# Turning the shared groups' last controls ahead of the sorted groups in a two-layer network kernel with a routed mixture of experts

## The chip, the core and the metric

The kernel runs on one core of a Trainium2 chip, as one program. The core's engines run side by side and meet at semaphores: TensorE (PE: matrix products and transposes into PSUM), VectorE (DVE), ScalarE (ACT: table functions), GpSimd (POOL: here it issues the indirect DMAs, which gather and scatter rows by an index) and SyncE (SP: here it issues all other DMAs, strictly in its program's order). The metric is the device time of one execution in microseconds (us).

## The reference

The input is 8 sequences of 512 tokens with 128 features. Four blocks follow each other, each added to its input: an attention, a gated feed-forward, a linear attention with three small MLPs, and a mixture of experts (`_L1_ffn_ref`). All of the change lies in the last:

```python
logits = gelu(xf @ router_w1 + router_b1) @ router_w2 + router_b2
topk_p, topk_i = top_k(softmax(logits), 2)            # of 8 experts, p renormalised
v, integrated = 0, xf
for _ in range(2):
    ctx = concat([integrated, v])
    x_sh, v_sh = inl(gelu(ctx @ shared_w1 + b) @ shared_w2 + b, integrated, v, mu)
    x_r, v_r   = sum over the token's 2 experts e of  p_e * inl(gelu(ctx @ w1[e] + b) @ w2[e] + b, integrated, v, mu)
    x_next, v_next = sw * x_sh + (1 - sw) * x_r, sw * v_sh + (1 - sw) * v_r
    halt = sigmoid(gelu(integrated @ halt_w1 + b) @ halt_w2 + b)
    integrated, v = integrated + halt * (x_next - integrated), v + halt * (v_next - v)
out = xf + integration_weight * (gelu(integrated @ refine_w1 + b) @ refine_w2 + b)

def inl(ctrl, x, v, mu):                              # ctrl: the three controls a, b, g of a token
    v_next = sigmoid(a) * v - softplus(b) * (x - mu)
    return x + 0.1 * sigmoid(g) * v_next, v_next
```

## The kernel before

The mixture works on groups of 512 tokens (four tiles of 128). A *shared* group S holds tokens in their own order and applies the shared weights; a *sorted* group E holds tokens that were scattered by expert into memory (`slots`), and each of its four tiles uses one expert's weights. The tokens are cut in two halves h = 0, 1, and there are two iterations it = 1, 2. `STAGES` sets the order of the 56 groups: S(h0,it1) 0 to 3, E(h0,it1) 4 to 13, S(h1,it1) 14 and 15, **E(h1,it1) 16 to 25**, S(h1,it1) 26 and 27, S(h0,it2) 28 to 31, **E(h0,it2) 32 to 41**, S(h1,it2) 42 to 45, **E(h1,it2) 46 to 55**. The three E stages in bold follow shared groups; `LATE_STARTS` holds their first groups, 16, 32 and 46. "Place 1", "2" and "3" below are the turns from shared to sorted groups at 16, 32 and 46.

A group passes these steps, and each engine runs its list of steps in an order written out by loops over `s`:

- SP `load_in` reads a sorted group's tokens from `slots` (the first three of a stage at once, as soon as the scatters of that half are through); `load_w1` reads its experts' first weights, four DMAs, and waits until the hidden layer of the sorted group four before has been through ACT (semaphore a_g); `store` writes a sorted group's results to `moved`.
- PE `g_turn` ("T") transposes the group's tokens, ACT `turned` copies them out of PSUM. PE `g_hidden` ("H") multiplies by the first weights, ACT `hidden_gelu` applies the gelu.
- PE `g_control` multiplies by the second weights: one or two units a group, in two pairs of PSUM banks used in turn, so that a unit waits for ACT to have read the unit before last. DVE `copy_b` copies the b controls out of PSUM and ACT `gates`, which waits for that copy, applies tanh to the others.
- ACT `soft` makes the softplus of the b controls of two groups at once. It is a table load, Exp, Ln and a second table load.
- DVE `elements` (waits for the softplus) and `moved_on` make the group's results. For a shared group they also write the token's own state.

Around this POOL moves rows. For each of the phases 0, 1 and 2 it runs over the 16 tiles of a half: `gather` (two indirect DMAs) fetches a token tile's two expert results from `moved`, DVE `update` adds them to the token's state, and `scatter` (two indirect DMAs) sends the new state to `slots` for the next sorted stage. Phase 0 begins once the results of all sorted groups to 13 are stored, phase 1 once those to 25 are. In the last stage `slots_back` sends sorted results back by index, four DMAs a group, and waits for that group's `moved_on`. `UPDATES` places the updates at the ends of DVE's steps s, from s = 16, 30 and 45 on.

`turn_steps(s)` says where in step s PE and ACT do which T and H. SP's loop is

```python
for s in range(-1, NG + 2):
    if is_e(s + 5):
        load_w1(s + 5)
        if not any(f <= s + 5 < f + 3 for f in LATE_STARTS):
            load_in(s + 5)
    if is_e(s - 2) and by_slots(s - 2):
        store(s - 2)
```

so at s = 15 it stands at `load_w1(20)`, `load_in(20)`, `store(13)`.

Of the kernel before, what the change touches and what calls it, by code (L numbers as in the profile page):

```python
# [96 lines left out]
GROUPS = []  # L97
# [9 lines left out]
def turned_in(g):  # L107

    return GROUPS[g][0] == "E" or GROUPS[g][2] == 2
# [34 lines left out]


LATE_STARTS = (16, 32, 46)


def dve_parts(g):
# [3 lines left out]

    if not turned_in(g) or g == FIRST_E or any(f <= g < f + 3 for f in LATE_STARTS) or GROUPS[g - 5][0] == "S" or GROUPS[g][2] == 2:
        return ()
# [7 lines left out]
def turn_steps(s):  # L163

    if s < FIRST_E:
        f = FIRST_E
        return [], [("T", f), ("T", f + 1), ("H", f), ("T", f + 2), ("H", f + 1)] if s == f - 1 else []  # L170
    turned = lambda g: g < NG and turned_in(g)
    middle = [("H", s + 2)] if turned(s + 2) and s + 2 not in LATE_STARTS and s + 1 not in LATE_STARTS else []
    end = [("T", s + 3)] if turned(s + 3) and s + 3 not in LATE_STARTS and s + 2 not in LATE_STARTS else []
    if s + 2 in LATE_STARTS:
        end = [("T", s + 2)]
    if s + 1 in LATE_STARTS:
        middle = [("H", s + 1)]
        end = [("T", s + 2), ("H", s + 2), ("T", s + 3)]
    return middle, end
# [76 lines left out]
def build(nc, x, early, late, experts, seconds, out):  # L256
    with ExitStack() as ctx:
# [538 lines left out]
        def _(dve):  # L796
# [209 lines left out]
            for t in range(NSEQ):  # L1006
                k, s = t % 2, with_b(t)
# [275 lines left out]
                r_norm(t)  # L1283
            weights(0)
            for s in range(1, NG + 2):
                if s < NG:
                    copy_b(s, 0)
                if s >= 2:
                    elements(s - 2)
                if s < NG:  # L1290
                    if unit_count(s) == 2:
                        copy_b(s, 1)
                if s >= 2:
                    moved_on(s - 2)
                if s == 2:
                    routes(1)
                    hots(1)
                if s == 3:
                    sort(1)
                if s == 4:  # L1300
                    weights(1)
                for what, g in turn_steps(s)[1]:
                    if what == "T":
                        turned(g)
                for ph, m in UPDATES.get(s, ()):
                    update(ph, m)
# [21 lines left out]
        def _(act):  # L1328
# [141 lines left out]
            for t in range(NSEQ):  # L1470
                k, s = t % 2, with_b(t)
# [131 lines left out]

            for s in range(NG + 1):
                middle, end = turn_steps(s)
                if s % 2 == 0 and s >= 2:
                    soft(s // 2 - 1)
                if s < NG:
                    gates(s, 0)
                if s == 1:  # L1610
                    r_gelu(HSEQ + 2)
                for what, g in middle:
                    hidden_gelu(g)
                if s < NG and unit_count(s) == 2:
                    gates(s, 1)
                if s == 0:
                    shares(0)
                    r_evacuate(HSEQ, 0)
                    r_evacuate(HSEQ + 1, 0)
                    r_gelu(HSEQ)  # L1620
                    r_evacuate(HSEQ + 2, 1)
                    r_gelu(HSEQ + 1)
                    r_evacuate(HSEQ + 3, 1)
                if s == 1:
                    r_gelu(HSEQ + 3)
                if s == 3:
                    shares(1)
                for what, g in end:
                    if what == "T":
                        turned(g)  # L1630
                    else:
                        hidden_gelu(g)
# [682 lines left out]
```

How the kernel before makes its waits and increments, by code:

```python
def need(eng, sem, value):  # L216
    if not isinstance(value, int) or value > 0:
        eng.wait_ge(sem, value)
# [2 lines left out]
def settle(eng, S):  # L222
    eng.wait_ge(S["row_in0"], 16)
# [242 lines left out]
        @block.sync  # L468
        def _(sp):
            for t in range(NSEQ // 2):
                sp.dma_start(X[:, 2 * t * TILES:2 * (t + 1) * TILES, :], x_in[t]).then_inc(S[f"row_in{t}"], 16)
            sp.dma_start(WE[:, FIRST_N:], early[:, FIRST_N:]).then_inc(S["w_early"], 16)
            sp.dma_start(WL[:, :], late).then_inc(S["w_late"], 16)
            sp.wait_ge(S["p_set"], 1)
            for d in (*X1d, *X2d):
                flat = d.rearrange("(p a) d -> p (a d)", p=P)
                for a in range(0, flat.shape[1], 4 * SEQ):
                    n = min(4 * SEQ, flat.shape[1] - a)
                    sp.dma_start(flat[:, a:a + n], zeros[:, 0:n]).then_inc(S["z_fill"], 16)
            sp.wait_ge(S["w_late"], 16)
            sp.wait_ge(S["z_fill"], 16 * (Z_FILLS - 1))
            sp.dma_start(X1d[1].rearrange("(p a) d -> p a d", p=P)[:, :, P], wl("spare"), allow_slow_non_contiguous=True)\
                .then_inc(S["z_fill"], 16)
            sp.wait_ge(S["ln_rs"], 14)
            sp.dma_start(EW2, seconds).then_inc(S["w_late"], 16)
            def experts_of(h, i):
# [5 lines left out]
            def load_in(g):  # L495
                _, h, it, i = GROUPS[g]
                e = EXP_AT[g]
                sp.wait_ge(SC[h], 16 * 2 * HT * it)
                if e == 4:
                    sp.wait_ge(S["r_y"], NSEQ)
```

## Time and profile before

| | us |
|---|---|
| median of 3 runs (991.86, 994.6, 995.5) | 994.6 |
| the profiled execution | 991.68 |
| its span | 989.9 |
| busy: PE, DVE, ACT, POOL | 782.1, 577.9, 566.4, 488.1 |
| busy share: PE, DVE, ACT, POOL | 79%, 58%, 57%, 49% |

The span is what the instructions cover; the 1.8 us beside it lie before the first and after the last. Every number of an instant counts from the span's start. No engine is busy throughout, so what counts is which one is waited for at each place.

### The profile page before, as it was taken

To read this page: it belongs to the slowest core of one execution; us is meant where nothing else is said; L and a number is where in the kernel's file an instruction comes from. 1 tells how busy PE (TensorE), PEld (TensorE's weight loads), DVE (VectorE), ACT (ScalarE), POOL (GpSimd) and SP (SyncE) were. 2 spreads that over 40 slices of the span, in tenths; PEclk is the share of its full clock that TensorE was granted. 3 is DMA by queue.
4 is the path that set the end of the run, shared out by engine and by line. 5 is a ranking of instruction groups with operands and counts; after the bars stand their busy time and mean duration, and the time that the engine had idled before them with its cause. 6 is when DMAs were issued, how large, how long until landed. Compare 5 with 4: busy or idle time off the path is not lost.

```text
span 989.9 us, 13034 instructions
## 1 busy us (share of the span) xinstructions
PE 782.1 (79%) x3904; PEld 535.8 (54%) x3904; DVE 577.9 (58%) x1438; ACT 566.4 (57%) x1003; POOL 488.1 (49%) x436
## 2 busy tenths in 40 slices
PE   7799997587888877999999856575576668877477
PEld 4588886444444435767676644454344444544255
DVE  6622333648888682222434588658566877586655
ACT  5744444544445304635544539877666898788532
POOL 1411202335554486224434777537777775467750
PEclk9999999799999997999999969887898999888789
DMA  9940000000000000000000535657557664633124
GB/s 344 423 136 1 0 1 1 1 1 0 1 1 1 0 1 0 1 1 1 1 1 27 186 92 152 207 158 226 166 175 238 202 191 146 196 121 101 48 78 128
DMA packets 75921, 92.90 MB, mean 94 GB/s; under 512 B 24032, under 2 KB 61920, under 8 KB 73808
## 3 DMA queue, kind: packets, MB, share of 16 engines
q1 hardware_dynamic: 65248, 65.87, 20.7%
q0 software_dynamic: 10464, 25.66, 8.1%
q10 hardware_dynamic: 144, 0.59, 0.2%
q8 instruction: 31, 0.51, 0.2%
q14 instruction: 34, 0.28, 0.1%
HBM read 45.95 MB, written 46.13 MB: 93 GB/s over the span
## 4 chain that ended last, share of the span: by engine, by line
PE 46%; DVE 16%; POOL 11%; ACT 11%; issue 9%; DMA 5%; POOLq 0%; DVEq 0%; SPq 0%; ACTq 0%
PE PS L1945 7%; PE PS L1954 6%; POOL tokens L693 4%; POOL KEEP L770 3%; PE PS L1752 3%; PE PS L1723 3%; PE PS L1864 3%; PE PS L1960 3%; PE PS L1832 3%; POOL slots L684 3%; PE PS L1713 2%; DMA KEEP<-moved,small 2%; DVE TEMP L961 2%; PE PS L1660 2%; PE PS L2058 2%
## 5 line engine op out<-in xcount | busy, mean ns | idle before, releaser
L2069 PE MATMUL PS<-TEMP,KEEP 128*128 x320 | 116.9, 508 | 36.9 <-ACT TEMP L1569 30.4
L770 POOL DMA_INDIRECT KEEP<-moved,small x96 | 104.4, 1087 | 69.9 <-issue 35.4
L675 POOL DMA_INDIRECT slots<-KEEP,small x96 | 101.1, 1053 | 47.2 <-issue 27.4
L2069 PEld LDWEIGHTS PS<-TEMP,KEEP 128*128 128x128 f32 x320 | 66.5, 223 | 65.1 <-issue 50.7
L1509 ACT ACTIVATE KEEP<-PS,TEMP 128x512 f32<-128x512 f32 x96 | 63.5, 690 | 58.0 <-PE PS L1945 57.1
L1569 ACT ACTIVATE TEMP<-PS 128x512 f32<-128x512 f32 (+2 forms) x92 | 51.5, 561 | 78.3 <-DVE TEMP L1180 77.7
L621 POOL TENSOR_TENSOR KEEP<-KEEP 128x1024 f32<-128x1024 f32 x32 | 63.7, 2005 | 53.6 <-PE PS L1864 51.8
L1945 PE MATMUL PS<-TEMP_R 128*128 128x512 f32 x288 | 77.1, 422 | 4.2 <-POOL TEMP_R L715 3.8
L2091 PE MATMUL PS<-KEEP,TEMP 128*64 128x128 f32 x480 | 40.2, 308 | 42.2 <-issue 19.1
L1864 PE MATMUL PS<-KEEP,TEMP 128*128 128x512 f32 x128 | 62.7, 619 | 9.3 <-DVE TEMP L961 8.2
L1945 PEld LDWEIGHTS PS<-TEMP_R 128*128 128x128 f32 x288 | 56.2, 198 | 20.1 <-POOL TEMP_R L715 4.2
L1180 DVE COPY TEMP<-PS 128x256 f32<-128x256 f32 (+1 forms) x92 | 43.8, 477 | 37.9 <-PE PS L2058 19.4
L2091 PEld LDWEIGHTS PS<-KEEP,TEMP 128*64 128x64 f32 x480 | 29.7, 154 | 64.4 <-issue 25.3
L1582 ACT ACTIVATE KEEP<-PS,TEMP 64x128 f32<-64x128 f32 x160 | 57.7, 360 | 9.4 <-PE PS L2091 7.6
L1954 PE MATMUL PS<-KEEP,TEMP 128*128 128x512 f32 x128 | 56.3, 593 | 0.0
L2058 PE MATMUL PS<-WL,KEEP 128*128 128x257 f32 (+1 forms) x128 | 47.7, 510 | 6.4 <-ACT TEMP L1569 6.3
L1666 PE MATMUL PS<-WL,TEMP 128*128 128x128 f32 x256 | 39.9, 297 | 16.0 <-DMA TEMP<-slots 13.1
L1273 DVE SCALAR_TENSOR_TENSOR KEEP<-KEEP,small 128x256 f32<-128x256 f32 (+1 forms) x64 | 26.5, 414 | 39.7 <-DMA KEEP<-moved,small 33.5
L1127 DVE TENSOR_SCALAR TEMP_R<-PS,TEMP 128x512 fp32r<-128x512 f32 x16 | 12.0, 751 | 62.3 <-PE PS L1954 62.3
L961 DVE TENSOR_TENSOR TEMP<-PS,KEEP 128x1024 f32<-128x1024 f32 x32 | 38.9, 1216 | 15.0 <-PE PS L1864 13.1
L1666 PEld LDWEIGHTS PS<-WL,TEMP 128*128 128x128 f32 x256 | 31.6, 151 | 27.8 <-issue 21.0
L715 POOL TENSOR_TENSOR TEMP_R<-KEEP,TEMP_R 128x512 fp32r<-128x512 f32 x8 | 8.7, 1090 | 73.3 <-ACT KEEP L1501 73.3
(275 smaller groups left out, 1877.5 us busy)
## 6 DMA issues: line engine op xcount, KB each, us to landing
slots<-LX SPq DMA_DIRECT2D x14, 1024.0 KB, 25.8
moved<-LX SPq DMA_DIRECT2D x20, 512.0 KB, 3.3
TEMP<-slots SPq DMA_DIRECT2D x20, 512.0 KB, 3.8
TEMP<-experts SPq DMA_DIRECT2D x80, 64.5 KB
TEMP<-seconds SPq DMA_DIRECT2D x1, 3072.0 KB
TEMP<-early SPq DMA_DIRECT2D x1, 2765.0 KB, 12.0
TEMP<-experts SPq DMA_DIRECT2D x80, 32.5 KB
TEMP<-slots SPq DMA_DIRECT2D x10, 258.0 KB, 3.8
```

The lines of the kernel that those rows point to most:

```text
L621: pool.tensor_tensor(o, kk, vv, ALU.mult).then_inc(S["c1_kv"], 1)
L675: pool.indirect_dma_start(dst, bass.IndirectOffsetOnAxis(ap=pos[:, h, 2 * m + k:2 * m + k + 1], axis=0), src, None).then_inc(SC[h], 16)
L770: pool.indirect_dma_start(G[:, n % 4, k, 0:w], None, src, bass.IndirectOffsetOnAxis(ap=pos[:, h, 2 * m + k:2 * m + k + 1], axis=0))\
L961: dve.tensor_tensor(qm[:, c % 2].rearrange("p (h v k) -> p h v k", h=HEADS, v=HD), acc, q, ALU.mult)\
L1509: act.activation(d_G[:, k, SEQ * c:SEQ * (c + 1)], PS[:, 2 + c, :], ACT.Gelu_apprx_tanh, bias=bias)\
L1666: last = pe.transpose(PS[:, bank, P * j:P * (j + 1)], src[:, j], eye)
L1864: last = pe.matmul(PS[:, 4 + 2 * (c % 2) + h, :], we("tril"), kv[:, c % 2, SEQ * h:SEQ * (h + 1)], start=True, stop=True)
L1945: last = pe.matmul(PS[:, 2 + c, :], CWr[:, pw, at:at + P], hTr[:, k, px], start=n == 0, stop=n == 2)
L1954: last = pe.matmul(PS[:, 6 + k, :], w2[:, P * c:P * (c + 1)], d_G[:, k, SEQ * c:SEQ * (c + 1)], start=c == 0, stop=c == HC - 1)
L2058: last = pe.matmul(PS[:, bank + j, 0:n], HS[:, hs_slot(g), col:col + P], wl("sw2")[:, 0:n], start=True, stop=True)
L2069: last = pe.matmul(o, hT[:, e % 3, P * j:P * (j + 1)], EW2[:, 384 * (j % 2):][:, bass.ds(at[j], n)], start=True, stop=True)
L2091: last = pe.matmul(PS[side:side + EHID, bank, part], W1[:, e % 4, j, 1 + EHID * a:1 + EHID * (a + 1)], xTs[:, x % 2, a, part], start=a == ...
```

## The change

At each late start f, the two shared groups f-2 and f-1 are finished before the sorted groups are turned. On ACT, `soft` of that pair moves from the start of step f into step f-1, behind the gates of group f-1. On DVE, `elements` and `moved_on` of f-2 and f-1, which stood in steps f and f+1 between the copies of sorted controls, stand at the start of step f ahead of those copies. At 16 and 32 (`TURNED_LAST`) T and H of the first sorted groups move behind both control units of group f-1 on PE and behind the softplus on ACT; at 46 T and H keep their places on PE, and on ACT the copy of 47 and what follows come behind the softplus. SP and POOL keep their lists word for word.

```diff
 LATE_STARTS = (16, 32, 46)
+TURNED_LAST = (16, 32)
...
     end = [("T", s + 3)] if turned(s + 3) and s + 3 not in LATE_STARTS and s + 2 not in LATE_STARTS else []
-    if s + 2 in LATE_STARTS:
+    if s + 2 in LATE_STARTS and s + 2 not in TURNED_LAST:
         end = [("T", s + 2)]
-    if s + 1 in LATE_STARTS:
+    if s + 1 in TURNED_LAST:
+        f = s + 1
+        if GROUPS[f][2] == 1:
+            end = [("T", f), ("T", f + 1), ("H", f), ("T", f + 2), ("H", f + 1)]
+        else:
+            end = [("T", f), ("H", f), ("T", f + 1), ("H", f + 1), ("T", f + 2)]
+    elif s + 1 in LATE_STARTS:
         middle = [("H", s + 1)]
         end = [("T", s + 2), ("H", s + 2), ("T", s + 3)]
...
             for s in range(1, NG + 2):
+                if s in LATE_STARTS:
+                    for g in (s - 2, s - 1):
+                        elements(g)
+                        moved_on(g)
+                in_turn = s >= 2 and s not in LATE_STARTS and s - 1 not in LATE_STARTS
                 if s < NG:
                     copy_b(s, 0)
-                if s >= 2:
+                if in_turn:
                     elements(s - 2)
                 if s < NG:
                     if unit_count(s) == 2:
                         copy_b(s, 1)
-                if s >= 2:
+                if in_turn:
                     moved_on(s - 2)
...
-                if s % 2 == 0 and s >= 2:
+                if s % 2 == 0 and s >= 2 and s not in LATE_STARTS:
                     soft(s // 2 - 1)
...
                 if s < NG and unit_count(s) == 2:
                     gates(s, 1)
+                if s + 1 in LATE_STARTS:
+                    soft(s // 2)
```

ACT at place 1, before. The first row is `gates` of group 14 (both units); L1599 is the copy of a turned group (16, 17, 18), L1582 the gelu of a sorted group (16, 17), the other 128x2x129 rows are the gates of group 15, and the last four rows are the softplus of 14 and 15.

```order
L1569 ACTIVATE TEMP<-PS 128x2x129 x2
L1599 ACTIVATE KEEP<-PS,WL 128x512
L1569 ACTIVATE TEMP<-PS 128x2x129
L1582 ACTIVATE KEEP<-PS,TEMP 64x128 x4
L1569 ACTIVATE TEMP<-PS 128x2x129
L1599 ACTIVATE KEEP<-PS,WL 128x512
L1582 ACTIVATE KEEP<-PS,TEMP 64x128 x4
L1599 ACTIVATE KEEP<-PS,WL 128x512
L1554 ACT_TABLE_LOAD
L1558 ACTIVATE LX<-TEMP 128x1024
L1560 ACTIVATE LX<-LX 128x1024
L1561 ACT_TABLE_LOAD
```

ACT at place 1, in the changed kernel, whose lines are 12 higher on this engine:

```order
L1581 ACTIVATE TEMP<-PS 128x2x129 x4
L1566 ACT_TABLE_LOAD
L1570 ACTIVATE LX<-TEMP 128x1024
L1572 ACTIVATE LX<-LX 128x1024
L1573 ACT_TABLE_LOAD
L1611 ACTIVATE KEEP<-PS,WL 128x512 x2
L1594 ACTIVATE KEEP<-PS,TEMP 64x128 x4
L1611 ACTIVATE KEEP<-PS,WL 128x512
L1594 ACTIVATE KEEP<-PS,TEMP 64x128 x4
```

The softplus has moved ahead of the first copy of a sorted group, and so ahead of the gelu of group 16 (the first row of four).

ACT at place 2, before: the first row is the gates of group 30, L1599 and L1601 are the two copies of a turned group of iteration 2 (32, then 33, then 34), the single 128x514 rows are the gates of group 31, and then comes the softplus of 30 and 31.

```order
L1569 ACTIVATE TEMP<-PS 128x514 x2
L1599 ACTIVATE KEEP<-PS,WL 128x512
L1601 ACTIVATE KEEP<-PS 128x512
L1569 ACTIVATE TEMP<-PS 128x514
L1582 ACTIVATE KEEP<-PS,TEMP 64x128 x4
L1569 ACTIVATE TEMP<-PS 128x514
L1599 ACTIVATE KEEP<-PS,WL 128x512
L1601 ACTIVATE KEEP<-PS 128x512
L1582 ACTIVATE KEEP<-PS,TEMP 64x128 x4
L1599 ACTIVATE KEEP<-PS,WL 128x512
L1601 ACTIVATE KEEP<-PS 128x512
L1554 ACT_TABLE_LOAD
```

The same place in the changed kernel:

```order
L1581 ACTIVATE TEMP<-PS 128x514 x4
L1566 ACT_TABLE_LOAD
L1570 ACTIVATE LX<-TEMP 128x1024
L1572 ACTIVATE LX<-LX 128x1024
L1573 ACT_TABLE_LOAD
L1611 ACTIVATE KEEP<-PS,WL 128x512
L1613 ACTIVATE KEEP<-PS 128x512
L1594 ACTIVATE KEEP<-PS,TEMP 64x128 x4
L1611 ACTIVATE KEEP<-PS,WL 128x512
L1613 ACTIVATE KEEP<-PS 128x512
L1594 ACTIVATE KEEP<-PS,TEMP 64x128 x4
```

All copies and gelus of the sorted groups 32 to 34 now stand behind both gates of 31 and behind the softplus.

DVE at place 2 in the changed kernel, from the last update of step 31 to the first copies of group 32 (L1280 and L1283 are an update, L1218 to L1229 `elements`, L1240 to L1253 `moved_on`, once for group 30; the same eight rows follow for 31):

```order
L1280 SCALAR_TENSOR_TENSOR KEEP<-KEEP,small 128x256
L1283 SCALAR_TENSOR_TENSOR KEEP<-KEEP,small 128x256
L1218 TENSOR_SCALAR small<-TEMP,small 128x4
L1220 SCALAR_TENSOR_TENSOR small<-TEMP,small 128x4 x2
L1222 SCALAR_TENSOR_TENSOR TEMP<-LX,TEMP 128x512
L1224 SCALAR_TENSOR_TENSOR TEMP<-TEMP,KEEP 128x4x128
L1229 TENSOR_TENSOR TEMP<-TEMP,KEEP 128x512
L1240 SCALAR_TENSOR_TENSOR LX<-TEMP 128x4x128
L1242 SCALAR_TENSOR_TENSOR LX<-TEMP,LX 128x4x128
L1253 SCALAR_TENSOR_TENSOR KEEP<-LX,small,KEEP 128x128 x4
```

What stood after `copy_b` of group 32 now stands ahead of it; ahead of all this, the update (1,0) at the end of step 30 still stands in front of `copy_b` of group 31, as before.

## Rows read from the trace of the kernel before

**Rows 1.** The chain that ended last: start, us, what; pieces at the three places.

```profile
640.34 3.25 DMA TEMP<-slots
...
652.22 4.08 DMA moved<-LX
...
657.11 1.45 POOL KEEP L770
...
751.32 1.94 PE PS L1666 x8
...
884.58 1.12 POOL tokens L693
```

**Rows 2.** POOL by stretches: us, busy (instructions), granted clock, DMA share, GB/s.

```profile
657.10:746.30 89.20, 69.97 (x64) 0.85 0.57 179
...
884.50:956.70 72.20, 56.19 (x53) 0.82 0.25 78
```

**Rows 3.** Timeline of ACT at place 1: start, us, instruction, idle before it.

```profile
640.21 0.89 ACT L1569 ACTIVATE TEMP<-PS 128x258 f32<-128x258 f32 x2
644.84 0.69 ACT L1599 ACTIVATE KEEP<-PS,WL 128x512 f32<-128x512 f32 x1 [3.74 <-PE PS L1666]
...
647.62 1.49 ACT L1582 ACTIVATE KEEP<-PS,TEMP 64x128 f32<-64x128 f32 x4 [0.22 <-PE PS L2091]
...
653.20 1.28 ACT L1554 ACT_TABLE_LOAD   x1
...
657.95 0.60 ACT L1569 ACTIVATE TEMP<-PS 128x512 f32<-128x512 f32 x1
```

**Rows 4.** Timeline of SP's DMA queue at place 1.

```profile
649.66 1.88 SPq L520 DMA_DIRECT2D TEMP<-experts  x4
...
652.22 0.61 SPq L527 DMA_DIRECT2D moved<-LX  x1
```

**Rows 5.** Timeline of PE at place 1.

```profile
635.49 1.14 PE L2058 MATMUL PS<-WL,KEEP 128*128 128x257 f32 x4 [0.36 <-ACT TEMP L1569]
643.72 1.08 PE L1666 MATMUL PS<-WL,TEMP 128*128 128x128 f32 x4 [7.09 <-DMA TEMP<-slots]
644.60 1.92 PE L2058 MATMUL PS<-WL,KEEP 128*128 128x257 f32 x4
```

**Rows 6.** Timeline of DVE at place 1.

```profile
649.01 0.68 DVE L1235 SCALAR_TENSOR_TENSOR LX<-TEMP,LX 128x512 f32<-128x512 f32 x1
```

**Rows 7.** Timeline of DVE at place 2.

```profile
754.21 0.48 DVE L1273 SCALAR_TENSOR_TENSOR KEEP<-KEEP,small 128x256 f32<-128x256 f32 x1 [2.01 <-DMA KEEP<-moved,small]
...
755.86 0.42 DVE L1180 COPY TEMP<-PS 128x256 f32<-128x256 f32 x1 [0.65 <-PE PS L2058]
...
757.68 0.68 DVE L1222 TENSOR_TENSOR TEMP<-TEMP,KEEP 128x512 f32<-128x512 f32 x1
```

**Rows 8.** Timeline of ACT at place 2.

```profile
756.32 0.60 ACT L1569 ACTIVATE TEMP<-PS 128x514 f32<-128x514 f32 x1 [2.43 <-DVE TEMP L1180]
...
762.25 1.49 ACT L1582 ACTIVATE KEEP<-PS,TEMP 64x128 f32<-64x128 f32 x4 [1.20 <-PE PS L2091]
...
774.76 0.60 ACT L1569 ACTIVATE TEMP<-PS 128x512 f32<-128x512 f32 x1 [1.26 <-DVE TEMP L1180]
...
778.99 1.28 ACT L1554 ACT_TABLE_LOAD   x1
```

**Rows 9.** Timeline of ACT at place 3.

```profile
857.70 0.69 ACT L1599 ACTIVATE KEEP<-PS,WL 128x512 f32<-128x512 f32 x1
...
877.15 1.28 ACT L1554 ACT_TABLE_LOAD   x1
```

**Rows 10.** Timeline of DVE at place 3.

```profile
866.24 0.23 DVE L1211 TENSOR_SCALAR small<-TEMP,small 128x4 f32<-128x4 f32 x1 [3.45 <-ACT TEMP L1560]
...
871.17 0.35 DVE L1273 SCALAR_TENSOR_TENSOR KEEP<-KEEP,small 128x128 f32<-128x128 f32 x1
...
880.62 0.69 DVE L1215 SCALAR_TENSOR_TENSOR TEMP<-LX,TEMP 128x512 f32<-128x512 f32 x1 [1.18 <-ACT LX L1560]
```

## The prediction

> **What bounds the kernel now.** The page comes first: no engine is over 79% busy, so an average decides nothing. The chain that ended last comes next, and at the three places it names what is waited for [rows 1]. At place 1 it goes from the first load of sorted tokens (640.34) over PE to the store of group 13 (652.22, 4.08 us to landing), and from there to POOL's first gather at 657.11. At place 2 it comes out of a load into T of group 32 (751.32) and then follows ACT and PE. In the last stage it enters POOL, whose first `slots_back` is at 884.58. The stretches of POOL say what lies between: 64 indirect DMAs in 89.2 us from 657.1 to 746.3, and 53 in 72.2 us from 884.5 to 956.7 [rows 2]. That is 1.39 and 1.36 us each; the timeline of POOL shows 0.30 us between neighbours and nothing longer in both stretches. POOL issues them as fast as it can. So whatever delays its first gather of phase 0, or its first `slots_back`, is paid at the end in full. Between 751 and 846 ACT, PE and DVE hand work to each other every few tenths; only a wait inside that round counts there. So the question is, place by place: when does the gelu of 16 end (place 1), when does ACT get to softplus (16) of groups 32 and 33 (place 2), and when to softplus (23) of 46 and 47 (place 3)?
>
> **Place 1.** PE waits 7.09 us for the sorted tokens [rows 5]. The change lets it do the units of group 15 in that time. The first waits for the gates of 14, which ACT begins at 640.21 and has done at 640.6 and 641.1 [rows 3]. A unit takes 1.14 us at the higher clock; a first one after a long idle time took 1.92 [rows 5]. The two end at 641.8 and 643.0, or at 642.6 and 644.4. T of 16 follows, its data landing at 643.7. DVE copies the b controls (0.42), does the two operations of `elements(13)` (1.4), copies again; the gates of 15 (0.39 each) end at 644.5 to 645.3. `moved_on(13)` ends near 645 to 645.9 and not at 649.01 + 0.68 = 649.7 [rows 6]. That is the gain that one sees first, 4 us or more.
>
> ACT, however, now does softplus (7) first: from 653.20 to 657.95 it took 4.75 us [rows 3]. So the copy of 16 starts at 649.3 to 650.0 and not at 644.84. It takes 0.69, H of 16 then takes 0.7 to 1.1 with its hand-overs, and the gelu 1.49: it ends at 652.2 to 653.5. Before it ended at 647.62 + 1.49 = 649.11. SP is queued behind that: `load_w1(20)` waits for this gelu and started 0.55 us after it, at 649.66, and behind it in SP's list stands `store(13)`, at 652.22 [rows 4]. SP's list is unchanged, so the result of 13 that is ready 4 us earlier lies there while SP waits 3.1 to 4.4 us longer for experts' weights that nobody needs yet. POOL's first gather waits for that store. It starts at 660.2 to 661.5. I take **+3.5 us**, since the clock falls part of the way. Nothing gives it back up to 746: POOL is full. The updates wait for gathers, so DVE and ACT come later by the same amount. What remains of DVE's freed time, the `elements` and `moved_on` of 15 out of the way of step 17, is worth nothing here, as POOL sets the pace.
>
> **Place 2**, counted from its own load. The units of 31 can run from 749.1 on, in the wait for the load at 751.32. But DVE's next act is not their copy. It is the update (1,0), which waits for a gather until 754.21, and its two operations end at 755.2 [rows 7]. `copy_b` of 31 started at 755.86 before, and starts at 755.2 now. The wait that the change wants to fill has another wait in front of it: it wins 0.6 us. From there I count ACT from the first gates of 31 to softplus (16).
>
> Before: from 756.32 to 778.99, 22.67 us [rows 8]. Its waits are 0.41, 0.45, 1.20 (for H), 1.26 (for DVE's copy) and 0.45, together 3.8 (the timeline gives each in brackets, the two longest are in the rows), so 18.9 is work. The 1.18 us of copies of 32 lay earlier, in a wait.
> After: it starts 755.7. The work is 18.9 + 1.18 = 20.1. The waits are: 1.8 from one gate of 31 to the other, since the `elements(29)` between the two copies hold DVE for 2.4 (from 755.86 to 757.68 + 0.6 in rows 7); 1.2 each for H of 32 and of 33, since nothing else stands between copy and gelu any more; 0.2 and 0.4 and 0.4 in step 32; 0.8, 0.1 and 0.5 in step 33, where DVE has no elements left. Together 6.6. It ends at 755.7 + 20.1 + 6.6 = 782.4: **+3.4 us**. DVE does not make it worse: `moved_on(29)` and the updates (1,1) and (1,2) end at 762.4, four blocks of 2.3 us for 30 and 31 follow, and `copy_b` of 32 is reached at 772, when PE gives it. PE idles near 10 us before H of 32. If it is then at the lower clock, as the L2058 of 1.92 us against 1.14 was [rows 5], H and T lose up to 1.5 us: upper end +5. At the lower end the small waits that I added vanish: +2.5. Nothing waits for a DMA in DVE up to 838, so no slack swallows it.
>
> **Place 3.** On ACT softplus (22) now begins where the copy of 47 did, at 857.70 [rows 9], and Ln is ready at 861.1. DVE then runs both groups at once: from `elements(44)` at 866.24 to its first update at 871.17 are 4.93 us with a copy of 0.34 in it [rows 10], so 4.7 a group; from 861.2 it is busy until 870.6, and only then copies the controls of 46, which PE had ready at 867.2. ACT before: from 857.70 to softplus (23) at 877.15 are 19.45 us [rows 9], with waits of 1.20, 1.61 and 0.45. After: the same work, with waits of 1.2 (H of 47), 3.6 (DVE's copy, from 867.5 to 871.05), 0.5 and 0.4. That is 5.7 against 3.3: **+2.4 us**, between +1.5 and +3.5. `elements(46)` started at 880.62 when Ln was there, and starts at 883.0. `moved_on(46)` ended at 884.2, and POOL's `slots_back(46)` followed at 884.58 [rows 1]: no slack. The gathers ahead of it on POOL wait for updates which keep their times.
>
> **Sum:** 3.5 + 3.4 + 2.4 = 9.3 us, and by the ends 3.1 + 2.5 + 1.5 = 7.1 to 4.4 + 5 + 3.5 = 12.9. A gain is excluded at place 1 by SP's order and at 2 by DVE's. Against the profiled execution's own 991.68 this is 1001.0. The median of the runs shown is 2.9 above that execution, whose time is their lowest; on the median the sum gives 1003.9. I take 1003.5.
>
> **A rule weighed.** A table load takes 1.28 us, and the softplus with two of them, Exp and Ln ends 4.75 us after it began, when the gates of 16 start [rows 3]; two drains would not fit into that. The Trainium skill (ScalarE: Activation LUTs, What ACT_TABLE_LOAD costs) adds a drain of about 1.38 us to every switch, 2.66 together. By that the softplus would be 7.5 us, and place 1 alone would cost 2.8 us more, a sum of 12.1. The row decides here.
>
> **Rivals.**
> 1. *The store is not held, so place 1 does not lose.* If SP reaches `store(13)` before the gelu of 16, because load and store stand otherwise than I read them or the first wait is met by other work, POOL starts when `moved_on(13)` is done: 4.7 us earlier and not 3.5 later. The sum is then 9.3 - 8.2 = +1.1, 995.7 on the median: no slower. For it speaks that the result is really earlier. Against it speak 649.66 right behind 649.11 and SP's unchanged list. It decides whether the first gather comes before or after 657.1 in the trace.
> 2. *The gather of update (1,0) lands before 751*, so that copies, gates and softplus (15) run in the wait for the load. ACT gets to the copy of 32 about 4.7 us earlier than I count, at 758.8, and place 2 gives -1.3. The sum is +4.6, 999.2 on the median. Against it: gathers and the first loads share the DMA engines there, and DVE waited 2.01 us for it [rows 7].
> 3. *The loss is larger:* PE's clock is lower at each restart, and at place 3 DVE's late copies also delay the updates ahead of POOL's gathers. All upper ends and 2 us for the gathers: +15, 1009.6.
> 4. *Everything is absorbed* or the freed engines win somewhere that I do not see, above all in DVE's steps 17, 33 and 47, which are shorter now by 4 to 5 us each. If two of these three reached the chain, some 9 us would come back and it would be level, or up to 5 us faster with all three.
>
> **How the numbers follow.** A measurement of this kernel tells about 0.5%, 5 us, from no change. The forecast (+7 to +13) has a chance of 0.64, rival 1 of 0.10, rival 2 of 0.08, rival 3 of 0.10, rival 4 of 0.07; the table rule has 0.01. Slower by over 0.5%: 0.64 + 0.10 + 0.01 and half of rival 2, 0.79. Within 0.5%: rival 1, half of 2, and 0.02 of 4, 0.16. Faster: 0.05. The range takes the forecast with the 3 us between single runs of one kernel and reaches to rivals 2 and 3: 997 to 1009.
>
> **What would show it.** POOL's first gather of `moved` at 660 to 661.5, with 64 DMAs behind it without a gap; SP's four expert loads straight after a gelu that ends at 652 to 653.5; `moved_on(13)` done near 645 and waiting. At place 2, ACT idle from the gates of 30 until some 4.4 us after T of 32 began, and softplus (16) 31 us after that T instead of 27.7. At place 3, DVE without a pause from Ln to the copy of 46, and 2.4 us more from the second gates of 45 to softplus (23). I am wrong if the first gather comes before 657 or if the stretches after it are shorter.

## The result, and the profile after

The changed kernel takes 1005.43 us (median of 4 runs, 1002.69 to 1009.32), the kernel before 995.05 us in the same comparison: a ratio of 1.0115, with a 95% interval of 1.0084 to 1.0146. The change costs some 11 us. The profiled execution took 1002.69 us with a span of 1000.9 us, so 11.0 us more than the one of before.

Place 1 first: SP's DMA queue of the changed kernel. These rows answer to [rows 4].

```profile
644.50 0.61 SPq L534 DMA_DIRECT2D moved<-LX  x1
655.33 1.88 SPq L527 DMA_DIRECT2D TEMP<-experts  x4
657.32 0.52 SPq L517 DMA_DIRECT2D TEMP<-slots  x1
657.89 0.62 SPq L534 DMA_DIRECT2D moved<-LX  x1
```

Between the stores of 12 and of 13 SP stands 10 us before the expert load of group 20. Its two neighbours on the timelines, ScalarE and VectorE of the changed kernel, say why, and what was ready meanwhile; they answer to [rows 3, 6].

```profile
646.63 1.28 ACT L1566 ACT_TABLE_LOAD   x1
...
651.38 1.26 ACT L1611 ACTIVATE KEEP<-PS,WL 128x512 f32<-128x512 f32 x2
653.29 1.49 ACT L1594 ACTIVATE KEEP<-PS,TEMP 64x128 f32<-64x128 f32 x4 [0.65 <-PE PS L2105]
...
665.96 0.60 ACT L1581 ACTIVATE TEMP<-PS 128x512 f32<-128x512 f32 x1 [9.08 <-DVE TEMP L1187]
```

```profile
646.11 0.68 DVE L1242 SCALAR_TENSOR_TENSOR LX<-TEMP,LX 128x512 f32<-128x512 f32 x1
...
662.10 0.69 DVE L1229 TENSOR_TENSOR LX<-TEMP,KEEP 128x512 f32<-128x512 f32 x1 [6.86 <-DMA moved<-LX]
...
665.24 0.69 DVE L1187 COPY TEMP<-PS 128x512 f32<-128x512 f32 x1
```

`moved_on(13)` is over at 646.8. The gelu of 16 comes behind softplus (7) and ends at 654.8. Only then does SP issue the expert load, then the load of 20, and at 657.89 the store of the result that has lain ready for 11 us. POOL's first gather waits for it, as the timeline and two stretches of POOL show (they answer to [rows 2]; columns: us, busy with instructions, granted clock of TensorE, DMA share, GB/s).

```profile
662.82 0.98 POOL L777 DMA_INDIRECT KEEP<-moved,small  x1 [25.18 <-DMA moved<-LX]
```

```profile
662.70:749.80 87.10, 67.67 (x64) 0.75 0.58 183
895.20:967.40 72.20, 55.84 (x53) 0.82 0.25 77
```

The reader is to see three things here. The first gather is 5.7 us later than before. The 64 DMAs behind it have no gap, but take 87.1 us and not 89.2. And there is a wait that the prediction does not have: `elements(15)` writes the buffer from which the store of 13 reads, so VectorE stands 6.86 us, and ScalarE behind it 9.08 us. It adds nothing to the chain: VectorE's first update, at 666.96, still waits 1.03 us for its gather.

Place 2, ScalarE and TensorE of the changed kernel, answering to [rows 8] and the T row of [rows 1]:

```profile
754.23 0.60 ACT L1581 ACTIVATE TEMP<-PS 128x514 f32<-128x514 f32 x1 [0.67 <-DVE TEMP L1187]
758.28 0.60 ACT L1581 ACTIVATE TEMP<-PS 128x514 f32<-128x514 f32 x1 [3.46 <-DVE TEMP L1187]
760.70 0.60 ACT L1581 ACTIVATE TEMP<-PS 128x514 f32<-128x514 f32 x1 [1.82 <-DVE TEMP L1187]
...
769.32 1.49 ACT L1594 ACTIVATE KEEP<-PS,TEMP 64x128 f32<-64x128 f32 x4 [2.07 <-PE PS L2105]
...
785.75 1.28 ACT L1566 ACT_TABLE_LOAD   x1
```

```profile
758.00 1.04 PE L1680 MATMUL PS<-WL,TEMP 128*128 128x128 f32 x8
767.29 1.97 PE L2105 MATMUL PS<-KEEP,TEMP 128*64 128x128 f32 x16 [8.26 <-ACT KEEP L1613]
...
791.83 2.66 PE L2083 MATMUL PS<-TEMP,KEEP 128*128 x4 [2.59 <-ACT TEMP L1581]
794.41 1.62 PE L2105 MATMUL PS<-KEEP,TEMP 128*64 128x128 f32 x16
```

Place 3, ScalarE, answering to [rows 9]:

```profile
865.83 1.28 ACT L1566 ACT_TABLE_LOAD   x1
...
873.83 1.49 ACT L1594 ACTIVATE KEEP<-PS,TEMP 64x128 f32<-64x128 f32 x4 [2.08 <-PE PS L2105]
...
879.24 0.60 ACT L1581 ACTIVATE TEMP<-PS 128x512 f32<-128x512 f32 x1 [2.72 <-DVE TEMP L1187]
...
887.96 1.28 ACT L1566 ACT_TABLE_LOAD   x1
```

Single executions of one kernel differ by several microseconds (35 runs of the kernel before on one chip: 990.3 to 1000.7), and part of that has arisen by 630 us, ahead of every edit: softplus (6) starts at 635.46 before and 636.80 after, and between 635.5 and 639.9 over all the kernels below, though nothing ahead of it differs. So I compare stretches between fixed points of the timelines, not absolute times. A is from softplus (6) to the first gather; B from there to the first gather of the second half; C to softplus (16); D to softplus (21); E to softplus (23). In us:

| profiled execution | A | B | C | D | E | ratio of times (95%) |
|---|---|---|---|---|---|---|
| before | 21.65 | 89.47 | 32.41 | 65.26 | 32.90 | |
| changed | 26.02 | 87.17 | 35.76 | 66.64 | 35.57 | 1.0115 (1.0084 to 1.0146) |
| place 1 alone | 26.24 | 86.37 | 31.83 | 65.27 | 31.51 | 1.0016 (0.9993 to 1.0040) |
| place 2 alone | 21.89 | 89.26 | 37.80 | 66.65 | 32.90 | 1.0052 (1.0033 to 1.0072) |
| place 3 alone | 22.77 | 88.13 | 32.62 | 65.27 | 35.58 | 1.0024 (0.9998 to 1.0050) |
| changed, store first | 15.97 | 88.76 | 37.57 | 66.55 | 35.55 | 1.0012 (0.9991 to 1.0033) |
| before, store first | 17.97 | 89.86 | 32.47 | 65.28 | 31.33 | 0.9960 (0.9936 to 0.9985) |
| changed, update (1,0) behind | 26.11 | 87.01 | 33.59 | 65.26 | 35.64 | 1.0087 (1.0054 to 1.0120) |
| changed, 18 fillers | 26.24 | 86.50 | 38.19 | 65.26 | 33.95 | 1.0113 (1.0081 to 1.0145) |
| changed, 10 fillers | 26.04 | 86.92 | 34.85 | 67.78 | 35.57 | 1.0122 (1.0085 to 1.0159) |
| place 3, softplus alone | 21.60 | 89.42 | 32.62 | 65.26 | 36.82 | 1.0029 (1.0007 to 1.0051) |
| place 3, VectorE alone | 21.76 | 89.53 | 32.45 | 65.31 | 39.51 | 1.0104 (1.0057 to 1.0150) |
| place 1 and store first | 16.71 | 88.66 | 31.88 | 65.30 | 31.35 | 0.9941 (0.9909 to 0.9973) |

From softplus (6) on the changed kernel's span is 9.66 us longer: A and B together 2.07, C 3.35, D 1.38, E 2.67, and what lies behind 0.19. The other 1.34 us of the 11.0 stand ahead of softplus (6).

### The profile page after: what moved, and what is told of

Read it like the earlier page. It is cut to its first block, busy times and chain, and to the rows that moved or that the text cites. A ratio compares the mean times of both kernels' runs of the same rounds, so it can differ in the third digit from the quotient of the medians.

```text
span 1000.9 us, 13034 instructions
## 1 busy us (share of the span) xinstructions
PE 794.6 (79%) x3904; PEld 544.6 (54%) x3904; DVE 579.5 (58%) x1438; ACT 567.0 (57%) x1003; POOL 484.5 (48%) x436
## 4 chain that ended last, share of the span: by engine, by line
PE 48%; DVE 16%; ACT 14%; issue 10%; POOL 9%; DMA 3%; SPq 0%; POOLq 0%; DVEq 0%; ACTq 0%
PE PS L1959 7%; PE PS L1968 6%; POOL tokens L700 4%; PE PS L1766 3%; PE PS L1737 3%; PE PS L1878 3%; POOL KEEP L777 3%; PE PS L1974 3%; PE PS L1846 3%; PE PS L2083 3%; PE PS L1727 2%; DVE TEMP L968 2%; ACT L1566 2%; DMA KEEP<-moved,small 2%; PE PS L1674 2%
## 5 line engine op out<-in xcount | busy, mean ns | idle before, releaser
L2083 PE MATMUL PS<-TEMP,KEEP 128*128 x320 | 123.2, 530 | 29.8 <-ACT TEMP L1581 25.4
L777 POOL DMA_INDIRECT KEEP<-moved,small x96 | 99.8, 1039 | 79.2 <-issue 36.3
L682 POOL DMA_INDIRECT slots<-KEEP,small x96 | 103.5, 1079 | 47.3 <-issue 26.8
L2083 PEld LDWEIGHTS PS<-TEMP,KEEP 128*128 128x128 f32 x320 | 69.1, 231 | 60.3 <-issue 46.5
L2105 PE MATMUL PS<-KEEP,TEMP 128*64 128x128 f32 x480 | 42.9, 324 | 53.4 <-ACT KEEP L1613 18.0
L2105 PEld LDWEIGHTS PS<-KEEP,TEMP 128*64 128x64 f32 x480 | 32.0, 164 | 75.6 <-ACT KEEP L1613 32.0
L1280 DVE SCALAR_TENSOR_TENSOR KEEP<-KEEP,small 128x256 f32<-128x256 f32 (+1 forms) x64 | 26.5, 414 | 38.0 <-DMA KEEP<-moved,small 32.1
L1878 PEld LDWEIGHTS PS<-KEEP,TEMP 128*128 128x128 f32 x128 | 22.6, 195 | 40.1 <-issue 30.9
L2072 PEld LDWEIGHTS PS<-WL,KEEP 128*128 128x128 f32 x128 | 27.4, 227 | 31.1 <-ACT TEMP L1581 18.2
## 6 DMA issues: line engine op xcount, KB each, us to landing
TEMP<-seconds SPq DMA_DIRECT2D x1, 3072.0 KB, 11.3
```

What stands on the lines that cost most here:

```text
L682: pool.indirect_dma_start(dst, bass.IndirectOffsetOnAxis(ap=pos[:, h, 2 * m + k:2 * m + k + 1], axis=0), src, None).then_inc(SC[h], 16)
L777: pool.indirect_dma_start(G[:, n % 4, k, 0:w], None, src, bass.IndirectOffsetOnAxis(ap=pos[:, h, 2 * m + k:2 * m + k + 1], axis=0))\
L1878: last = pe.matmul(PS[:, 4 + 2 * (c % 2) + h, :], we("tril"), kv[:, c % 2, SEQ * h:SEQ * (h + 1)], start=True, stop=True)
L2072: last = pe.matmul(PS[:, bank + j, 0:n], HS[:, hs_slot(g), col:col + P], wl("sw2")[:, 0:n], start=True, stop=True)
L2083: last = pe.matmul(o, hT[:, e % 3, P * j:P * (j + 1)], EW2[:, 384 * (j % 2):][:, bass.ds(at[j], n)], start=True, stop=True)
L2105: last = pe.matmul(PS[side:side + EHID, bank, part], W1[:, e % 4, j, 1 + EHID * a:1 + EHID * (a + 1)], xTs[:, x % 2, a, part], start=a == ...
```

## Experiments

**One place at a time.** The three parts of the change (order of transposes, VectorE's elements, softplus) get a list of places each; for place 1 alone all three hold 16, for place 2 alone 32, and for place 3 alone the first is empty and the other two hold 46.

```diff
-TURNED_LAST = (16, 32)
+TURNED_LAST = (16,)
+DVE_FIRST = (16,)
+SOFT_FIRST = (16,)
...
-                if s in LATE_STARTS:
+                if s in DVE_FIRST:
                     for g in (s - 2, s - 1):
...
-                in_turn = s >= 2 and s not in LATE_STARTS and s - 1 not in LATE_STARTS
+                in_turn = s >= 2 and s not in DVE_FIRST and s - 1 not in DVE_FIRST
...
-                if s % 2 == 0 and s >= 2 and s not in LATE_STARTS:
+                if s % 2 == 0 and s >= 2 and s not in SOFT_FIRST:
...
-                if s + 1 in LATE_STARTS:
+                if s + 1 in SOFT_FIRST:
```

> The new order at the start at group 16 alone; the starts at 32 and 46 as before. Theory of the store (the expert load that waits for the gelu of 16 stands ahead of the store of 13 in SP's queue, and the first gather waits for that store): the gelu of 16 ends 3 to 4.5 us later, the first gather is issued 4 to 5 us later than in the kernel before, POOL gives back about 2 us of it over the 64 gathers and scatters, as the changed kernel's trace shows, and the loads of 32 to 34 and the end come 2.5 to 4 us later: about 998.4 us. Rival, the clock (the longer silences of TensorE at a start bring it down to its lower level, and most of the 10 us comes from that at 32 and 46): nothing of place 1 reaches the end, 995 us. Before group 16 nothing differs; if softplus stands 1.3 us late from 600 us on here as well, that offset belongs to something else than the order.

Measured: 995.04 against 994.16 us, 1.6 us by the ratio, and not told apart from nothing. That is the time of the rival and not the 998.4 of the theory. The theory's own sign is there: A is 4.6 us longer, as expected. But B is 3.1 us shorter where 2 had been expected, so of the loss at the store 1.5 us are left, and in this execution even those are covered, by C (0.6 shorter) and by E (1.4 shorter, because TensorE's clock was higher there; see the last section).

> The new order at the start at group 32 alone. Theory of the blocked copies (the copy of 31 waits on VectorE behind the first update of the second half, and the copies, gelu and softplus of 32 wait behind it on ScalarE): softplus of pair 16 starts 3.4 us later than before, counted from the landing of the loads of 32, and with some matmuls at the lower clock behind it up to 1.4 us more is lost before the gates of 44: 998 to 1000 us. Rival (the loss at 32 is only there because place 1 moved the gathers and so the landing of the first update against the gates): the loss is under 1.5 us here, below 996.5.

Measured: 999.92 us, 5.2 us by the ratio. The loss at 32 is there without place 1, and it is larger than in the changed kernel's trace: C by 5.4 us, where 3.4 had been expected, and D by 1.4.

> The new order of softplus and VectorE's elements at the start at group 46 alone; TensorE's order is the one before everywhere. Theory: from the second gates of 45 to softplus of pair 23 it takes 2.4 to 2.7 us more and POOL's last part is bound by what it gets from VectorE: 997.3 to 998 us. Rival (the last part is bound by POOL's issues, which give the 2.5 us back): 995 us.

Measured: 998.11 us, 2.4 us by the ratio, at the edge of what can be told from nothing; E is longer by 2.68. The three single losses add up to 9.2 us, inside the interval of the whole change (8.4 to 14.5).

**The store ahead of the expert load**, in the changed kernel and in the one before:

```diff
             for s in range(-1, NG + 2):
+                if s == 15:
+                    store(s - 2)
                 if is_e(s + 5):
...
-                if is_e(s - 2) and by_slots(s - 2):
+                if is_e(s - 2) and by_slots(s - 2) and s != 15:
                     store(s - 2)
```

> The changed kernel, with one step moved in SP's program: at turn 15 the store of group 13 is issued ahead of the expert load of group 20 (which waits for the gelu of 16) and of the load of 20. Theory of the store: it is issued right behind moved_on of 13, near 647 us instead of 657.9, the first gather follows near 652 instead of 662.8, VectorE's wait of the elements of 15 for the store's landing is gone, and the end moves by 8 to 11 us: 994.5 to 997.5 us. Rival (the late restart of TensorE and ScalarE at 16 is what costs, and the gathers only follow it): no gain, 1004 to 1006 us, whatever the store does. Between these, about 1001 us, if the first updates are then waited for by something else.

Measured: 995.74 us, ratio 1.0012 to before; that is 10 us less than the changed kernel (6.9 us less in the profiled execution, counted from softplus (6)). The timeline of POOL:

```profile
652.29 1.05 POOL L781 DMA_INDIRECT KEEP<-moved,small  x1 [13.74 <-DMA moved<-LX]
```

The first gather is 10.5 us earlier than in the changed kernel. The gelu of 16 is not: in both kernels it ends 18.0 us behind the start of softplus (6). So a late gelu makes late gathers only through SP's order, which holds the finished store behind the load that waits for that gelu; this is shown. Places 2 and 3 still lose: D and E as in the changed kernel, C 5.2 us against the kernel before, more than the 3.35 of the changed kernel and near the 5.4 of place 2 alone.

> The kernel before, with the same step moved in SP's program as in the run of the changed kernel with the store first: at turn 15 the store of 13 ahead of the expert load of 20. Theory of the store: the expert load's wait for the gelu of 16 held the store in the kernel before too, so the first gather comes near 652 us instead of 657.1, and the 64 gathers and scatters behind it end about 6 us earlier: 987 to 990 us. Rival (the sorted groups' own chain takes over as soon as POOL is ready sooner): 992 to 994 us.

Measured: 991.97 against 994.15 us, ratio 0.9960. That is the time of the rival: A is shorter by 3.7 us, and 5 had been expected. SP now waits for something else, as its timeline and VectorE's show:

```profile
647.10 1.44 SPq L519 DMA_DIRECT2D TEMP<-slots  x1
648.59 3.54 SPq L536 DMA_DIRECT2D moved<-LX  x2
652.70 1.90 SPq L529 DMA_DIRECT2D TEMP<-experts  x4
```

```profile
648.80 0.42 DVE L1191 COPY TEMP<-PS 128x256 f32<-128x256 f32 x1 [5.64 <-PE PS L2076]
...
651.09 0.68 DVE L1246 SCALAR_TENSOR_TENSOR LX<-TEMP,LX 128x512 f32<-128x512 f32 x1
```

The row x2 of SP joins the stores of 12 and 13. With the old order `moved_on(13)` ends at 651.8, since VectorE waits for control products of 15 that stand behind T of 16. The new order removes just that. Hence the next kernel.

**Place 1 in the new order, and the store first**: both diffs above together, 32 and 46 as in the kernel before.

> Both edits that the stretch at group 16 seems to want: the new order at the start at 16 alone (as in the run of place 1 alone) and SP's store of 13 ahead of the expert load of 20. Theory of the store: the new order has the last elements of 13 done 5 us earlier than the old one does (646 against 651 us), and only SP's order kept that from the gathers; so the first gather comes 16 us behind softplus of pair 6 (before 21.7, store first alone 18.0), the first gather of the second half 6 us earlier than before, and with the old order at 32 and 46 nothing of it is given back: 987 to 989 us, ratio 0.993 to 0.995. Rival (the place loses as much by TensorE's silence as the store gains): as with the store first alone, 992 us, ratio 0.998.

Measured: 988.27 against 994.87 us, ratio 0.9941: faster than the kernel before and the changed one. A and B together are 105.4 us (before 111.1, changed 113.2, store first alone 107.8). By these stretches one part of the change is a gain of 2.5 us, once SP lets it through. The times alone do not show that part: the intervals of this kernel and of the store first alone overlap (0.9909 to 0.9973, and 0.9936 to 0.9985).

**The update behind the copy of 31**, in the changed kernel:

```diff
-        UPDATES.setdefault(_at + ((_m + 1) // 2 if _ph == 2 else UPDATE_STEPS[_m]), []).append((_ph, _m))
+        UPDATES.setdefault(_at + ((_m + 1) // 2 if _ph == 2 else max(UPDATE_STEPS[_m], _ph == 1)), []).append((_ph, _m))
```

> The changed kernel, with one step moved on VectorE: the first update of the second half stands behind the copy of 31 (turn 31) instead of ahead of it (turn 30). Theory of the blocked copies: the copy of 31 no longer waits for the landing of that update's gather, the second wait of the gates of 31 loses most of its 3.5 us, TensorE's silence before the hidden product of 32 shrinks from 8.3 us to about 5, and softplus of pair 16 comes 3 to 4.5 us earlier against the first gather of that half (35.8 us behind it in the changed kernel): 1000.5 to 1002 us. Rival (order of softplus and copies on ScalarE alone costs the 3.4 us): no change, 1005 us.

Measured: 1000.53 us, ratio 1.0087, some 3 to 5 us less than the changed kernel. Timelines of ScalarE and TensorE:

```profile
755.90 0.60 ACT L1583 ACTIVATE TEMP<-PS 128x514 f32<-128x514 f32 x1 [2.23 <-DVE TEMP L1189]
```

```profile
765.05 1.98 PE L2107 MATMUL PS<-KEEP,TEMP 128*64 128x128 f32 x16 [6.17 <-ACT KEEP L1615]
```

C falls by 2.2 us, where 3 to 4.5 had been expected, and the second gates of 31 still wait 2.23 us of the 3.46. Of the 3.35 us 1.2 are left; H of 32 still takes 1.98 us, at the lower clock. And D falls back to 65.26, which I had not expected of this edit: the silence of TensorE is 2.1 us shorter, and the pairs behind stand 13.48 us apart again.

**The clock.** Over 786 to 842 us TensorE was granted full clock before, and 0.91 of it in the changed kernel. At H of 32 and the T behind it (767.29 to 771.20) it was granted 0.50, the lower of its two levels, 1.2 of 2.4 GHz. The stretch by windows, before and after (columns: us, busy with instructions, granted clock, DMA share, GB/s):

```profile
786.00:842.00 56.00, 43.56 (x227) 1.00 0.59 178
```

```profile
786.00:842.00 56.00, 45.99 (x236) 0.91 0.56 170
```

To test it I filled the silence ahead of H of 32 with work whose result is overwritten. It writes the bank of H of 32, once the gelus that read the bank are done.

```diff
+FILLED, FILLERS = (("H", 32),), 18
...
+            def filler(g):
+                x = HID_AT[g]
+                pe.wait_ge(S["a_g"], x - 1)
+                for _ in range(FILLERS):
+                    pe.matmul(PS[:, 2 + x % 2, 0:384], wl("gA"), wl("sw2")[:, 0:384], start=True, stop=True)
...
                 for what, g in end:
+                    if (what, g) in FILLED:
+                        filler(g)
```

> The changed kernel with 18 matmuls of 128 x 384 added on TensorE between the transposes and the hidden product of group 32, into a bank that the product overwrites; the output does not change. They take 7 us at the higher clock and fill most of the silence of 8.3 us. Theory of the clock (the silence brings TensorE to its lower level, the products of 32 and 33 take 1.97 instead of 1.09 us, and for four pairs of groups behind it the first control products take 2.7 to 2.9 instead of 1.55 us): these rows go back to 1.09 and 1.55 us, softplus of pairs 16 to 20 stand 13.5 us apart as before instead of 14.0, and 2 to 3.5 us come back: 1002 to 1003.5 us. Rival (the clock is off the path; the distance is set by VectorE's updates): 1005 us, and 14.0 us apart whatever the clock.

Measured: 1005.25 us, as the changed kernel. TensorE's timeline:

```profile
761.52 11.78 PE L2139 MATMUL PS<-WL 128*128 128x384 f32 x36
773.22 1.09 PE L2108 MATMUL PS<-KEEP,TEMP 128*64 128x128 f32 x16
```

The clock did what was expected: H takes 1.09 us, the pairs are 13.48 apart and D is 65.26. So D's 1.38 us are the clock's. But the 18 fillers took 11.8 us and not 7 (each shows as two records of 0.33 us), and the gelu of 32 waited 3.87 us for them instead of 2.07. C grew by 2.4 us, 1.8 of it that wait, which is more than D gave back.

> The changed kernel with 10 added matmuls between the transposes and the hidden product of group 32 in place of 18 (18 took 11.8 us, ran 3.6 us past the moment at which the product could start, and gave back in the clock what they cost). 10 take 6.5 us, inside the silence of 8.3 us. Theory of the clock: nothing is delayed, the products of 32 and 33 take 1.09 us, the pairs behind stand 13.5 us apart; softplus of pair 16 comes 34 us behind the first gather of the second half, not 35.8, and that of pair 21 another 65.3 us behind, not 66.6: 1001.5 to 1003.5 us. Rival (the lower clock at 32 costs only where it shows, under 1 us in all): 1004.5 us or more.

Measured: 1006.32 us, a time that the rival had given; nothing came back. The fillers took 6.6 us and delayed nothing, C is 0.9 us shorter, but D is 1.1 longer. TensorE's timeline at the second pair of sorted groups:

```profile
792.91 1.57 PE L2086 MATMUL PS<-TEMP,KEEP 128*128 x4 [2.58 <-ACT TEMP L1584]
795.43 1.98 PE L2108 MATMUL PS<-KEEP,TEMP 128*64 128x128 f32 x16 [0.95 <-ACT KEEP L1616]
797.33 2.93 PE L2086 MATMUL PS<-TEMP,KEEP 128*128 x4
```

H of 32 ran at the higher clock (1.09 us), but the clock fell all the same, 26 us behind it (granted 0.50 over 795.4 to 800.3), and that one pair took 15.75 us. The clock theory holds for what a low stretch costs (1.4 us in D, 0.9 in C). That filling most of the long silence is enough to save it is wrong. The 18 fillers, which left nothing of it, did keep the clock up to 842; each size was profiled once.

**Place 3 taken apart.** Softplus ahead, VectorE as before (`SOFT_FIRST = (46,)`, the others empty):

> At the start at group 46 softplus of pair 22 goes ahead on ScalarE as in the changed kernel, but VectorE keeps the order of before; the starts at 16 and 32 are those of before. Theory (the loss of 2.4 to 2.7 us at this start is VectorE's, which does both groups' elements ahead of the copy of 46): no loss here, within 1 us of before, 993.5 to 995.5 us, and softplus of pair 23 comes 33 us behind that of 21, not 35.6. Rival (it is ScalarE's order, softplus ahead of the copies of 46 and 47, which leaves TensorE silent): 35.6 us again, 996.5 to 998 us.

Measured: 997.09 us, ratio 1.0029; E is 36.82. My theory fell. It is not VectorE's order that costs: softplus ahead of the copies costs 3.9 us of E by itself. (By the times it is 2.9 us, 0.7 to 5.1.) ScalarE's timeline has the waits that this order brings, for H of 47 at the lower clock and then for two copies of VectorE:

```profile
867.76 1.49 ACT L1596 ACTIVATE KEEP<-PS,TEMP 64x128 f32<-64x128 f32 x4 [2.08 <-PE PS L2107]
...
872.32 0.60 ACT L1583 ACTIVATE TEMP<-PS 128x512 f32<-128x512 f32 x1 [1.87 <-DVE TEMP L1189]
...
878.96 0.60 ACT L1583 ACTIVATE TEMP<-PS 128x512 f32<-128x512 f32 x1 [2.34 <-DVE TEMP L1189]
```

VectorE ahead, softplus as before (`DVE_FIRST = (46,)`, the others empty):

> At the start at group 46 VectorE does the elements of 44 and 45 ahead of the copy of 46, but softplus of pair 22 stays behind the copies, gelus and gates on ScalarE where it was; 16 and 32 as before. Theory formed on the last run (softplus ahead of the copies of 46 and 47 is what costs here, 3.9 us by itself, and VectorE's order gives 1.2 us of that back): alone VectorE's order gains nothing, since its elements wait for the late softplus and the copy of 46 waits behind them: softplus of pair 23 comes 35 to 38 us behind that of 21 (before 32.9): 996.5 to 999 us. Rival (VectorE's order is the better one whatever ScalarE does): 31.5 to 33 us and 993 to 994.5 us.

Measured: 1003.68 us, ratio 1.0104, E 39.51: worse than expected. The copy of 46 waits behind elements that wait for a late softplus, and ScalarE stands 8.61 us:

```profile
876.98 0.60 ACT L1583 ACTIVATE TEMP<-PS 128x512 f32<-128x512 f32 x1 [8.61 <-DVE TEMP L1189]
```

In E the two halves cost 3.9 and 6.6 us alone and 2.7 together. VectorE's order pays only when softplus has gone ahead; then it returns 1.2 of softplus's 3.9. The 3.9 and the 2.7 compare like with like: in the kernel before, with softplus alone ahead and in place 3 alone the same first products ran at the lower clock (2.94 us). With VectorE alone ahead they took 1.56 us, so the 6.6 is not taken at equal clock.

## Why the prediction was right, point by point

The forecast, slower by 9.3 us and 1003.5, stands beside 1005.43, in its range; the 9.66 us behind softplus (6) stand beside the 9.3. That the two meet so closely is partly luck: place 1 came out 1.4 us smaller than its term, and D, for which there was no term, added 1.4.

- **Place 1, the mechanism: right, and shown.** With the store ahead of the expert load the first gather came at 652.29. Rival 1 had priced just this case at 995.7 us, and 995.74 was measured, with luck in the closeness: A came out shorter than it had reckoned and C longer. It is not what the changed kernel does. The first gather at 662.82 lies behind the forecast 660.2 to 661.5 by the 1.3 us that stand ahead of softplus (6).
- **Place 1, the size: 3.5 forecast, 2.1 in the trace** (1.5 with place 1 alone). A is 4.4 us longer, where 3.1 to 4.4 were forecast; B is 2.3 shorter. That is one of the prediction's own signs of being wrong ("if the stretches after it are shorter"). The failing step is "nothing gives it back up to 746: POOL is full". POOL is full, but its issues are no constant: from the first gather to the first scatter, ten gathers later, it took 14.75 us before (657.11 to 671.86) and 12.81 in the changed kernel (662.82 to 675.63). Starting later does not explain it: with place 1 and store first they start 5 us earlier against softplus (6) than before and take 13.3. What goes with it in every trace is how busy VectorE is beside these ten. Busy 7.1 to 7.3 us, they take 12.6 to 12.8 us (the changed kernel, place 1 alone, the fillers, the update behind). Busy 9.4 and 10.3, they take 13.3 and 13.4 (place 1, and the changed kernel, with the store first). Busy 11.3 to 13.4, they take 14.0 to 14.75 (all kernels with the old order at 16). Before, `elements` and `moved_on` of 14 and 15 ran beside these gathers; the new order takes them away from there. No kernel changes this alone, so it is not shown as the cause.
- **"What remains of DVE's freed time ... is worth nothing here": probably wrong.** If the last point holds, this freed time is what B gave back, 1.9 of its 2.3 us within those ten gathers. And the 4 us by which `moved_on(13)` is ready earlier, worth nothing behind SP's list, count once that list is mended: with the store first A and B together are 105.4 us in the new order at 16 and 107.8 in the old.
- **Place 2: 3.4 forecast, 3.35 in C.** The copies do wait behind the update (1,0), as moving it shows (2.2 of the 3.35). The 1.82 us between the gates of 31 are the 1.8 that was forecast. But the waits for H of 32 were 2.07 and not 1.2, the lower clock that stood only at the upper end; other waits that were added came out shorter. The check "31 us after that T" does not apply: T of 32 no longer starts with its load but behind the controls of 31, at 758.00. Counted from 3.58 us behind SP's issue of the loads, as before, it is 31.0 us. Alone, place 2 costs 5.4 us in C: TensorE was silent for 9.7 us there and stayed at the lower clock for the products of 33 too, and behind them the gates of 32 waited 1.44 us for VectorE's copy. So the 3.35 depend on what the clock does, and their nearness to 3.4 is not proof of each term.
- **Missed: D, 1.38 us.** The prediction ended place 2 at softplus (16). The lower clock goes on for three more pairs, each 0.3 to 0.6 us longer. This is a part of rival 3, whose time of 1009.6 was too high.
- **Place 3: 2.4 forecast, 2.67 in E**; the sum of waits is right (2.08, 2.72, 0.52 and 0.45, together 5.8; forecast 1.2, 3.6, 0.5 and 0.4, together 5.7), but its story put the loss on VectorE's bunching. That wait is real: VectorE works without a pause from 869.31 and copies the controls of 46 at 878.79, 0.9 us behind TensorE's last product of them. But the bunching also takes away a later wait (2.34 us with softplus alone ahead). The halves show that the order of softplus is the cost and the bunching a partial cure.
- **"The gathers ahead wait for updates which keep their times": right.** POOL has issued them by 891.7 and waits 3.56 us for `moved_on(46)`. `slots_back(46)` follows at 895.27, 10.7 us later than before, and the 53 DMAs behind it take 72.2 us as before.
- **The table rule:** softplus (7) takes 4.75 us with its two loads in the changed kernel too (646.63 to 651.38), as in [rows 3]; the two loads and the two functions in it take 4.68. The drain that the Trainium skill adds (ScalarE: Activation LUTs, What ACT_TABLE_LOAD costs) does not show.

What stays open: whether VectorE's work is what lengthens POOL's issues, by an experiment, and where the 1.3 us ahead of softplus (6) come from, which no edit touches.

## What to carry to other kernels

When a result is ready earlier, look at the list of the queue that has to send it off: one load that nobody needs yet, but that waits for the engine which the edit makes later, turned a gain of 2.5 us (with the store first) into a loss of 2.1. Test a change of order by its places and halves: here the part at place 1 was a gain behind a single moved line, and the two halves of place 3 cost 10.5 us alone and 2.7 together. An engine that issues without a gap need not do so at a constant pace: compare the durations of its issues before you count a delay in full. And end a stretch of your sum not at the next familiar point, but where clock and pace are as before.

## What the runs showed of the hardware

The length of a silence of TensorE does not by itself tell the level at which the work behind it runs. At place 3 the same rows, with the same silence ahead of them, ran at either level from one kernel to another, though no edit lay within 100 us. TensorE's timeline of the kernel before, and of the one with place 1 alone:

```profile
849.65 2.94 PE L2058 MATMUL PS<-WL,KEEP 128*128 128x385 f32 x4 [2.94 <-ACT TEMP L1569]
```

```profile
852.39 1.56 PE L2074 MATMUL PS<-WL,KEEP 128*128 128x385 f32 x4 [2.93 <-ACT TEMP L1583]
```

The granted clock of these stretches (third number from the right), again before and place 1 alone:

```profile
849.65:853.00 3.35, 3.35 (x8) 0.50 0.46 159
```

```profile
852.39:855.70 3.31, 2.54 (x20) 1.00 0.49 163
```

The stretch E is 32.9 us in the one and 31.3 to 31.5 in the other and in both kernels with the old order there and a moved store. So 1.4 to 1.6 us of a difference between two kernels can lie in where the dips of the clock fall; that has to be read from the durations of equal rows before it is put down to an edit.

POOL's issue of an indirect DMA is longer in places where VectorE works beside it. POOL, then VectorE, in the kernel before with the store first:

```profile
656.59 0.96 POOL L781 DMA_INDIRECT KEEP<-moved,small  x1 [0.30 <-issue]
657.86 0.95 POOL L781 DMA_INDIRECT KEEP<-moved,small  x1 [0.30 <-issue]
659.11 1.49 POOL L781 DMA_INDIRECT KEEP<-moved,small  x1 [0.30 <-issue]
```

```profile
658.81 0.23 DVE L1222 TENSOR_SCALAR small<-TEMP,small 128x4 f32<-128x4 f32 x1 [2.30 <-ACT LX L1576]
659.09 0.68 DVE L1226 SCALAR_TENSOR_TENSOR TEMP<-LX,TEMP 128x512 f32<-128x512 f32 x1
659.81 0.69 DVE L1233 TENSOR_TENSOR LX<-TEMP,KEEP 128x512 f32<-128x512 f32 x1
```

The 13 traces have 832 issues in their stretches of 64 behind the first gather. Of these 111 lie wholly in a pause of VectorE, and none took over 1.00 us, whether ScalarE was busy or not. Of the other 721, beside which VectorE worked, 312 took longer, up to 1.49. So work of VectorE goes with a longer issue, but does not always bring it; that it is the cause was not tested by a run.
